# A perceiver block's cross-attention: the order of scores, maxima and projections within a double unit

## The reference

```
q = (LN(x) @ Wq + bq) per head;  k = (context @ Wk + bk);  v = (context @ Wv + bv)
attn = softmax(q k^T / 4 over all 12544 context tokens);  x = x + (attn v) @ Wo + bo
```

## Time and profile before

| | |
|---|---|
| time, median of 3 runs | 1286.22 us (1282.94 to 1286.94) |
| the profiled execution | 1283.76 us |
| its span | 1281.9 us |
| PE, DVE, ACT, POOL busy | 89%, 57%, 55%, 16% |
| mean granted TensorE clock | 0.959 |

### The profile page before, as it was taken

The page is one execution under the profiler, slowest core; times in us unless marked ns, Lnnn a source line. Parts: engine busy times, 40 slices in busy tenths (PEclk is TensorE's granted clock), DMA queues, the critical chain, the costliest instruction groups (busy, mean ns, idle before and its releaser), DMA issues.

```text
span 1281.9 us, 30526 instructions
## 1 busy us (share of the span) xinstructions
PE 1140.6 (89%) x13043; PEld 744.5 (58%) x13043; DVE 726.4 (57%) x1356; ACT 711.3 (55%) x1387; POOL 202.3 (16%) x114
## 2 busy tenths in 40 slices
PE   7899999999999999717799999999999999999777
PEld 4355566565556565517696355655565556665565
DVE  2566566665566664488323556665666666665343
ACT  3356666666666657352212356666666666667422
POOL 0222222222121110000000222222121222220000
PEclk9799999999999999857999799999999999999889
DMA  9544444443344350440905735443344444360360
GB/s 211 137 116 116 116 116 105 99 114 100 99 104 116 84 175 3 151 146 1 321 8 117 186 85 125 111 106 100 97 112 116 110 109 103 80 166 3 131 222 5
DMA packets 83929, 144.92 MB, mean 113 GB/s; under 512 B 9993, under 2 KB 73361, under 8 KB 83281
## 3 DMA queue, kind: packets, MB, share of 16 engines
q1 hardware_dynamic: 82896, 142.85, 42.1%
q10 hardware_dynamic: 896, 0.12, 0.1%
HBM read 64.64 MB, written 0.15 MB: 51 GB/s over the span
## 4 chain that ended last, share of the span: by engine, by line
PE 68%; ACT 13%; DVE 13%; issue 3%; DMA 2%; SPq 0%; ACTq 0%; DVEq 0%
PE ring L542 37%; PE st L542 15%; PE ot L542 14%; ACT work L995 6%; DVE mpart L1260 5%; ACT arena L960 2%; ACT arena L978 2%; DVE arena L1399 1%; PE ring L692 1%; ACT work L1001 1%; DMA arena<-rows 1%; DMA wkv<-L_wkv 1%; SPq L386 0%; DMA qst<-rowb 0%; DMA warena<-ctxT 0%
## 5 line engine op out<-in xcount | busy, mean ns | idle before, releaser
L1260 DVE TENSOR_REDUCE mpart<-ring 128x1 f32<-128x448 f32 x896 | 536.0, 621 | 352.5 <-PE ring L542 344.7
L995 ACT ACTIVATE work<-st 128x512 f32<-128x512 f32 x784 | 404.6, 601 | 156.2 <-PE st L542 156.0
L542 PE MATMUL ring<-arena,qst 96*128 96x448 bf16 x896 | 312.6, 369 | 44.8 <-ACT arena L960 20.7
L542 PE MATMUL ot<-work,arena 128*17 128x128 f32 x6272 | 233.7, 276 | 8.9 <-ACT work L995 1.9
L542 PE MATMUL st<-qst,arena 97*128 97x128 bf16 x3136 | 237.6, 219 | 1.5 <-DMA qst<-rowb 1.5
L542 PEld LDWEIGHTS st<-qst,arena 97*128 97x128 bf16 x3136 | 206.2, 98 | 42.4 <-issue 7.5
L503 POOL TENSOR_TENSOR arena<-arena 128x896 f32<-128x896 f32 x52 | 98.1, 1887 | 644.1 <-ACT arena L967 643.8
L542 PEld LDWEIGHTS ot<-work,arena 128*17 128x17 f32 x6272 | 142.0, 97 | 85.3 <-ACT work L995 51.2
L542 PEld LDWEIGHTS ring<-arena,qst 96*128 96x128 bf16 x896 | 83.2, 97 | 183.9 <-issue 81.9
L542 PE MATMUL ring<-wkv,warena 64*128 64x256 f32 (+1 forms) x784 | 155.7, 395 | 3.9 <-ACT arena L978 3.2
L542 PE MATMUL ring<-warena,wkv 128*128 128x448 f32 x448 | 151.8, 578 | 2.7 <-DMA warena<-ctxT 1.3
(11 more groups left out here) (281 smaller groups left out, 651.5 us busy)
## 6 DMA issues: line engine op xcount, KB each, us to landing
arena<-arena SPq DMA_DIRECT2D x336, 224.0 KB, 3.6
arena<-ffn_W SPq DMA_DIRECT2D x16, 1024.0 KB, 13.1
warena<-ctxT SPq DMA_DIRECT2D x28, 448.0 KB, 3.8
warena<-ctxT SPq DMA_DIRECT2D x56, 224.0 KB, 4.5
arena<-f SPq DMA_DIRECT2D x2, 4096.0 KB, 25.1
arena<-scratch_bc SPq DMA_DIRECT2D x1, 2048.0 KB, 7.1
arena<-rows SPq DMA_DIRECT2D x1, 1792.0 KB, 6.9
warena<-w_in_proj SPq DMA_DIRECT2D x1, 1024.0 KB
```

The costliest lines, as they stand in the source:

```text
L542: return nc.tensor.matmul(o, l, r, start=start, stop=stop, **kw)
L995: nc.scalar.activation(pbuf[:, n % 2, half * 512:(half + 1) * 512], st[:, 2 * (n % 2) + half], ACT.Exp).then_inc(*signal(f"{lay}_exp_done"))
L1260: V.reduce_max(mpart[:, 2 * h + hf:2 * h + hf + 1], ring[:, BANKS[step][0], 0:HALF], AX_X).then_inc(*signal(f"{lay}_b_max"))
```

## The change

Only the order of steps within a double unit changes. Before, a quarter of the maxima (rounded down) comes ahead of the first scores, a quarter between the two score steps, a quarter behind them, then the pair of key or value steps if the double has one, and then the remaining maxima. Now both score steps come first, then all maxima but one, then the pair, then the last maximum. In a double without a pair (`made` is False, or 0) all maxima follow the scores. The number of steps of each kind in a double, their limits and all else are the same.

```diff
--- before.py
+++ after.py
@@ -145,13 +145,14 @@
                 plan.append(("ot", c, 0))
             limit = c + 1 if w < 4 else c + 2
             n = per_pair[w]
-            plan += some(n // 4, limit) + score(c * UNITS + 2 * w + 2) + some(n // 4, limit)
-            plan += score(c * UNITS + 2 * w + 3) + some(n // 4, limit)
+            made = (w in values and c + 2 < NCH) or (w in keys and c + 3 < NCH)
+            plan += score(c * UNITS + 2 * w + 2) + score(c * UNITS + 2 * w + 3)
+            plan += some(n - 0 - made, limit)
             if w in values and c + 2 < NCH:
                 plan += [("v", c + 2, k) for k in values[w]]
             if w in keys and c + 3 < NCH:
                 plan += [("k", c + 3, k) for k in keys[w]]
-            plan += some(n - 3 * (n // 4), limit)
+            plan += some(made, limit)
             if w == 1 and c:
                 plan.append(("o", c - 1, 0))
             if c == 0 and w < 3:
```

## The result

The changed kernel takes 1366.53 us (median of 4 runs, 1362.95 to 1368.59) against 1285.43 before (median of 4): a ratio of 1.063, with an interval of 1.061 to 1.065. It is slower, by 81 us; 1369 was forecast. The profiled execution took 1365.45 us (span 1363.6), which is 81.7 over that of before, where the forecast said 84.

What follows compares the result with a forecast made beforehand. PE was taken as the bound, hardly kept waiting. 3.27 us per steady chunk gave 41.9 per layer, 84 for two; 1283.8 + 84 = 1368, or 1370 by the median; 1369 predicted, own range 1355 to 1385, wider range 1340 to 1405.

Steps and rivals of the forecast that it cites:

- The bound: Steady attention chunk: PE busy 32.5 of 34.4 us and hardly ever kept waiting; DVE never holds it there.
- The front: Start of a double: fourth maximum at 1.98 us behind the first matmul after pv (not 1.50), what follows at 2.51.
- Doubles without a pair: Doubles w1 and w4 of a steady chunk, without key or value pair: +0.79 us (to 4.09) and +0.57 (to 3.72).
- Doubles with a pair: Doubles w0, w2, w3, w5 of a steady chunk, with value or key pairs: +0.32, +0.32, +0.27, +0.33 us.
- its two terms: Doubles with a pair: front +1.13 us; gain behind the pair from the removed stall, -0.80 to -0.86.
- w6: Last double of a chunk, no pair: ACT reaches the copy of ot late; +0.14 to +0.67 us, 0.67 taken.
- Chunk 0: First chunk of a layer: eight maxima to most doubles, more of them behind DVE; 4 us taken.
- The rival of the falling clock: New waits idle PE in every double and lower its clock, twice a chunk: 55 us more, 1424; chance 0.12.
- Chunks 11 and 12: Late chunks of a layer: 11 has no key pairs, 2.5 us; 12 has maxima but no pairs, 2.7 us.
- Half the stalls: Rival: bank releases come sooner or pv hides part of them, so half of the loss: 1327; chance 0.05.
- not slower: Rival: the three banks absorb the maxima and pair doubles keep their gain of about 0.81 us: 1209; chance 0.04.
- The signal by which the forecast would have been wrong: In a double: the fourth maximum's matmul going before 1.8 us behind the first matmul after pv.

Runs made afterwards that it cites:

- e5: Changed kernel with each maximum taken over the first 224 of its 448 columns and 60 added to the joined maximum: 1287.73 us.
- e6: Kernel before with each maximum taken over the first 224 of its 448 columns and 60 added to the joined maximum: 1273.74 us.
- e3: Changed kernel, but with the order of before in the doubles without a pair: 1331.61 us, ratio 1.035.
- e1: Kernel before with both score units first and the rest as before, two maxima still behind a pair: 1383.91 us, ratio 1.075.
- e2: Kernel before with only one maximum behind the pair, maxima and scores still interleaved: 1259.94 us, ratio 0.980.

## Why the prediction was right

The bound: PE's in-order queue with DVE one step off it. Right, by e5 and e6: with DVE's step shortened, 67 of the 81 us that the change costs are gone.

The front: fourth maximum at 1.98, what follows at 2.51. Right to a hundredth, in doubles of both kinds. PE's own idle time is 0.34 and 0.17 there.

Doubles without a pair: w1 4.09 and w4 3.72 were forecast and measured. By e3 all doubles without a pair cost 35 us; the forecast has 1.36 us in each of chunks 1 to 10 and 2.7 in chunk 12, 33 us for two layers, and small parts of chunks 0 and 11.

Doubles with a pair: +0.32, +0.32, +0.27, +0.33 forecast; +0.31, +0.32, +0.27, +0.32 measured. e1 and e2 show its two terms with their signs: +98 us for the scores alone, -26 for the pair and its single maximum alone. They don't add up (72, not 81): the maximum that is moved ahead of the pair delays the pair by 0.23 with the interleaving (1.49 to 1.72), and by 0.54 behind two score units side by side (1.97 to 2.51).

w6: the mechanism right, the size off. The term was 0.67 and measured 0.51 (3.65 against 3.14). The step took the copy of ot to start when the cast ended, 0.80 behind P, and the first exp a whole copy later. It started at 0.70, and the exps 0.48 behind it: ACT's instructions overlap by about 0.1 in the record. This is 0.16 us in some 20 chunks, 3 us of the 84.

Chunk 0: taken as 4 with no sum behind it, measured 7.2 in the first layer. The double units of the second layer last what the waits alone give (its chunk 43.6, 4.2 over 39.4), so 3 us are the clock. The rival of the falling clock was right for two or three stretches of a first chunk, and wrong for the steady chunks, whose clock is 1.00. The prediction argued against it with a reading that was wrong: that the trace of before has no fall with waits under 1 us. Ahead of the first chunk it has one:

```profile
40.78 12.24 PE L542 MATMUL ring<-arena,qst 96*128 96x448 bf16 x23 [0.17 <-DVE mpart L1260]
```

From 37 us on PE had done one maximum per 0.53 us, idle for 0.17 us ahead of most of them, and the clock, 1.00 up to 40 us, is 0.50 from 41 us on; the last of these groups is shown. The first chunk after the change has the same pattern for seven or eight maxima at a time. The Trainium skill's page "TensorE: Matmul & The Clock Gate", section "A second HAM failure mode: psum-queue depth-cycling", describes TensorE swinging between its two clocks when it idles a little between groups of matmuls while it cycles through PSUM banks. It agrees in part: the clock swung behind some runs of seven and eight maxima, and not with the single waits of 0.34 and 0.17 us in the steady chunks, where PE cycles through the same banks.

Chunks 11 and 12: 2.5 and 2.7 forecast, 2.3 and 2.0 measured. The low clock that the kernel before had at 479 to 482, behind its wait of 1.46 us for the row, is absent after; there the wait is 0.84, since the later w4 and w5 cover more of that transfer.

The first layer's total is 42.0 us against 41.9 forecast, and that is luck: chunks 1 to 10 cost 30.5 where 32.7 were forecast (w6 is most of the difference), chunk 0 cost 7.2 where 4 was, and the errors cancel.

Half the stalls, and not slower: neither happened. The signal by which the forecast would have been wrong, a fourth maximum ahead of 1.8, is what e5 made by shortening the reduction, and there most of the loss went. DVE's busy time was to stay and fell by 31 us; that is the overlap in the record, not less work.

## What to carry to other kernels

In an in-order queue with few banks (three here; no other number was tried), work that another engine must empty is to be spaced by that engine's interval. Grouping it costs its first latency plus one interval per further step, even if that engine is only 60% busy. Ask of each pair of moves which one pays: here the single maximum behind the pair was worth 26 us and the scores side by side cost 98; together they hid that one half was an improvement. When a stall is taken out, see which in-order queue reached its next item just in time before, as ACT did for w6.

## What the runs showed of the hardware

Reductions of 448 columns take 0.61 to 0.62 us each but follow each other every 0.53; of 224 columns 0.38 and 0.30. A float32 pair whose first weight load could not run ahead took about 0.1 more (3.06 against 2.95 for values, 2.72 against 2.62 for keys). In four of the eight first chunks of a layer that have the change's order around the pairs, the clock fell to its lower level, 1.2 GHz, for some us at a time, after PE had done runs of maxima of 0.19 at one per 0.53 us; in the steady chunks, with four or five maxima to a double, it stayed at 1.00.
